# Two attention stages of a six-layer decoder kernel: fewer value products on TensorE, more copies on ScalarE, and a bias row added by GpSimd

## The reference

```python
# L0 self-attention: 16 heads of 64, one key and one value head shared by all of them
q = (x @ Wq) -> 16 heads; k, v = split(x @ Wkv)
out = softmax(q k^T / 8 + relative_bias, causal) v @ Wout + bout
# L0 cross-attention: 16 heads of 8 over ctx_1024 of the same sequence
q = x @ Wq + bq; k = ctx @ Wk + bk; v = ctx @ Wv + bv
out = softmax(q k^T / sqrt(8) + mask) v @ Wo + bo
```

## Time and profile before

| | |
|---|---|
| median of 3 runs | 2577.37 us (2576.12 to 2579.46) |
| the profiled execution | 2579.07 us |
| span of its trace | 2577.2 us |
| granted TensorE clock, mean | 0.947 |
| PE busy | 2276.2 us (88%) |
| DVE busy | 1941.7 us (75%) |
| ACT busy | 1413.3 us (55%) |
| POOL busy | 1165.4 us (45%) |

### The profile page before, as it was taken

The page is one execution under the profiler, slowest core; times in us unless marked ns, Lnnn a source line. Parts: engine busy times, 40 slices in busy tenths (PEclk is TensorE's granted clock), DMA queues, the critical chain, the costliest instruction groups (busy, mean ns, idle before and its releaser), DMA issues. The chain is left out here.

```text
span 2577.2 us, 89949 instructions
## 1 busy us (share of the span) xinstructions
PE 2276.2 (88%) x33769; PEld 1843.9 (72%) x33775; DVE 1941.7 (75%) x5469; ACT 1413.3 (55%) x3541; POOL 1165.4 (45%) x1038
## 2 busy tenths in 40 slices
PE   7999999989999871337999899998999999999975
PEld 7888888866666650126888678886888888888863
DVE  3777777758888878897888667775777777777765
ACT  1566666645665642346888678885444444444432
POOL 0333333326666642008999689994222222222222
PEclk9999999998999995758999999999999999999998
DMA  4000000000000000000000000000000000000002
GB/s 117 2 0 0 0 0 0 0 5 20 17 17 17 17 9 1 0 20 15 0 0 0 1 2 0 0 0 6 8 7 6 6 6 6 5 6 6 6 2 65
DMA packets 56164, 25.52 MB, mean 10 GB/s; under 512 B 17347, under 2 KB 55558, under 8 KB 56070
## 3 DMA queue, kind: packets, MB, share of 16 engines
q1 hardware_dynamic: 52658, 23.06, 3.3%
q10 hardware_dynamic: 3412, 1.19, 0.2%
HBM read 20.04 MB, written 4.19 MB: 9 GB/s over the span
## 5 line engine op out<-in xcount | busy, mean ns | idle before, releaser
L705 POOL TENSOR_TENSOR sa_sc<-sa_sc,sa_rs 128x1024 f32<-128x1024 f32 x64 | 121.9, 1904 | 338.0 <-DVE sa_rs L681 338.0
L1748 POOL TENSOR_TENSOR lo_qk_r<-lo_qk_ms,w_neg_half 128x20 f32<-128x20 f32 x64 | 226.9, 3546 | 22.5 <-DVE lo_qk_ms L1671 22.5
L1748 POOL TENSOR_TENSOR gl_qk_r<-gl_qk_ms,w_neg_half 128x20 f32<-128x20 f32 x64 | 226.8, 3544 | 1.1 <-DVE gl_qk_ms L1671 1.0
L947 POOL TENSOR_TENSOR xa_sc<-xa_sc,xa_rs 128x1024 f32<-128x1024 f32 x64 | 121.7, 1902 | 157.8 <-DVE xa_rs L923 157.8
L484 POOL TENSOR_TENSOR xan_ve<-xan_mv,w_eps_ln 128x1 f32<-128x1 f32 x64 | 13.3, 208 | 392.8 <-DVE xan_mv L478 392.8
L851 ACT ACTIVATE xan_xT<-xa_misc 128x128 f32<-128x128 f32 x64 | 17.8, 279 | 268.7 <-PE xa_misc L763 268.7
L784 PEld LDWEIGHTS xa_qs<-xan_xT,late_x_wq 128*128 128x128 f32 x1024 | 119.1, 191 | 52.6 <-issue 52.6
L920 DVE TENSOR_REDUCE xa_sm<-xa_sc 128x16 f32<-128x1024 f32 x64 | 78.1, 1220 | 89.2 <-ACT xa_sc L863 89.2
L678 DVE TENSOR_REDUCE sa_sm<-sa_sc 128x16 f32<-128x1024 f32 x64 | 78.1, 1220 | 82.0 <-ACT sa_sc L636 82.0
L560 PE MATMUL sa_qs<-san_xT,w_a_wq 128*128 128x128 f32 x1024 | 134.6, 286 | 1.7 <-DVE sa_sc L667 1.7
L784 PE MATMUL xa_qs<-xan_xT,late_x_wq 128*128 128x128 f32 x1024 | 131.3, 281 | 0.0
(11 more groups left out here) (330 smaller groups left out, 6833.4 us busy)
## 6 DMA issues: line engine op xcount, KB each, us to landing
w_x<-in_x_dram SPq DMA_DIRECT2D x8, 512.0 KB, 7.6
ca_cx<-in_ctx_dram SPq DMA_DIRECT2D x64, 64.0 KB, 1.8
xa_cx<-in_ctx_dram SPq DMA_DIRECT2D x64, 64.0 KB, 1.8
out_dram<-la_out SPq DMA_DIRECT2D x16, 256.0 KB, 2.3
ca_mask<-in_mask_BxSxS_ff_dram SPq DMA_DIRECT2D x64, 32.0 KB, 1.7
w_a_wq<-in_L_attn_Wq_dram SPq DMA_DIRECT2D x1, 512.0 KB
w_a_wo<-in_L_attn_Wout_dram SPq DMA_DIRECT2D x1, 512.0 KB
prep_xwo<-in_L_xattn_Wo_dram ACTq DMA_DIRECT2D x1, 512.0 KB
```

The source lines that it names most:

```text
L705: pool.tensor_tensor(v, v, bcast(rs[:, s, :], 2, S), ALU.mult).then_inc(prob_done, 1)
L947: pool.tensor_tensor(v, v, bcast(rs[:, s, :], 2, S), ALU.mult).then_inc(prob_done, 1)
L1748: pool.tensor_tensor(qk_r[:, s, :], qk_ms[:, s, :], k["neg_half"][:, 0:NQK], ALU.pow).then_inc(sg["qk_r"], 1)
```

## The change

Self: the two swapped value products go. ACT copies the values as they are, then copies each half of the rows into the other half; three activations with 64 elements in a row in place of one with 128, and the semaphore v counts three a tile.

Cross: the four value products become one over all 128 rows. ACT spreads it into both halves: four activations with 64 elements in place of two with 128. The bias row is no longer a product on PE; GpSimd adds it to x ahead of time into a new buffer `xb` (`copy_x`, lag 6, last in its order), and DVE's residual adds the output product to that.

The loops stay where the shorter or longer code ahead of them puts them. The diff, cut to the lines that change and a few around them:

```diff
@@ -537,7 +537,7 @@
                     after(pe, k_done, t, 1)
-                    after(pe, v_done, t, 1)
+                    after(pe, v_done, t, 1, per=3)
                     pe.transpose(misc[:, 0:P], norm["xn"][:, s, :], ident).then_inc(norm["xT_psum"], 1)
@@ -545,11 +545,7 @@
                     pe.matmul(misc[:, P:2 * P], k["a_wkk"][:, :, :].rearrange("p a b -> p (a b)"), xT[:, s, :], start=True, stop=True)
-                    pe.matmul(misc[:, 2 * P:2 * P + DH], xT[:, s, :], k["a_wv"][:, :], start=True, stop=True)
-                    for r in range(2):
-                        last = pe.matmul(misc[r * 64:r * 64 + 64, 2 * P + DH:3 * P], xT[:, s, (1 - r) * 64:(2 - r) * 64],
-                                         k["a_wv"][:, :], start=True, stop=True)
-                    last.then_inc(kv_psum, 1)
+                    pe.matmul(misc[:, 2 * P:2 * P + DH], xT[:, s, :], k["a_wv"][:, :], start=True, stop=True).then_inc(kv_psum, 1)
@@ -585,7 +581,7 @@
                 def attend(t, four):
-                    after(pe, v_done, t)
+                    after(pe, v_done, t, per=3)
@@ -621,7 +617,10 @@
                     after(act, o_psum, t, 4)
-                    act.activation(vx[:, four, :, :].rearrange("p a d -> p (a d)"), misc[:, 2 * P:3 * P], ACT.Copy).then_inc(v_done, 1)
+                    act.activation(vx[:, four, 0, :], misc[:, 2 * P:2 * P + DH], ACT.Copy).then_inc(v_done, 1)
+                    for r in range(2):
+                        act.activation(vx[r * 64:r * 64 + 64, four, 1, :], misc[64 - r * 64:128 - r * 64, 2 * P:2 * P + DH],
+                                       ACT.Copy).then_inc(v_done, 1)
@@ -973,6 +972,7 @@
+        xb = sb("xb", [P, 2, D])
@@ -1014,14 +1014,10 @@
-                    after(pe, v_done, t, 1, per=2)
+                    after(pe, v_done, t, 1, per=4)
                     pe.matmul(m2[:, 0:P], k["c_wq"][:, :], xcT[:, s, 0:P], start=True, stop=True)
                     pe.matmul(m2[:, P:2 * P], k["c_wk"][:, :], xcT[:, s, P:2 * P], start=True, stop=True)
-                    for b in range(2):
-                        for r in range(2):
-                            last = pe.matmul(m2[r * 64:r * 64 + 64, (2 + b) * P:(3 + b) * P], xcT[:, s, P + b * 64:P + b * 64 + 64],
-                                             k["c_wv"][:, :], start=True, stop=True)
-                    last.then_inc(qkv_psum, 1)
+                    pe.matmul(m2[:, 2 * P:3 * P], xcT[:, s, P:2 * P], k["c_wv"][:, :], start=True, stop=True).then_inc(qkv_psum, 1)
@@ -1038,7 +1034,7 @@
                 def attend(t, four):
-                    after(pe, v_done, t, per=2)
+                    after(pe, v_done, t, per=4)
@@ -1066,8 +1062,7 @@
-                    pe.matmul(m1[:, 2 * P:3 * P], oT[:, s, :], k["c_wo"][:, :], start=True, stop=False)
-                    pe.matmul(m1[:, 2 * P:3 * P], k["ones"][0:1, :], k["c_row"][0:1, :], start=False, stop=True).then_inc(y_psum, 1)
+                    pe.matmul(m1[:, 2 * P:3 * P], oT[:, s, :], k["c_wo"][:, :], start=True, stop=True).then_inc(y_psum, 1)
@@ -1096,10 +1091,10 @@
                     for r in range(2):
-                        rows = slice(r * 64, r * 64 + 64)
-                        act.activation(vz[rows, four, :, :, :].rearrange("p b c (q w) -> p b (c q) w", q=2)[:, :, :, r * HD:r * HD + HD],
-                                       m2[rows, 2 * P:4 * P].rearrange("p (b n e d) -> p b n e d", b=2, e=2, d=HD)[:, :, :, r, :],
-                                       ACT.Copy).then_inc(v_done, 1)
+                        for b in range(2):
+                            act.activation(vz[r * 64:r * 64 + 64, four, b, :, :].rearrange("p c (q w) -> p (c q) w", q=2)[:, :, r * HD:r * HD + HD],
+                                           m2[b * 64:b * 64 + 64, 2 * P:3 * P].rearrange("p (n e d) -> p n e d", e=2, d=HD)[:, :, r, :],
+                                           ACT.Copy).then_inc(v_done, 1)
@@ -1146,8 +1141,10 @@
                 def residual(t, four):
+                    s = four % 2
                     after(dve, y_psum, t)
-                    dve.tensor_tensor(tile_of(X, t), m1[:, 2 * P:3 * P], tile_of(X, t), ALU.add).then_inc(x_done, 1)
+                    after(dve, xb_done, t)
+                    dve.tensor_tensor(tile_of(X, t), m1[:, 2 * P:3 * P], xb[:, s, :], ALU.add).then_inc(x_done, 1)
@@ -1174,7 +1171,11 @@
-                skewed(pool, NT, [(4, shift), (0, rsqrt), (2, blocks)], 4)
+                def copy_x(t, four):
+                    after(pool, x_done, t, 2)
+                    pool.tensor_tensor(xb[:, four % 2, :], tile_of(X, t), k["c_row"][:, :], ALU.add).then_inc(xb_done, 1)
+
+                skewed(pool, NT, [(4, shift), (0, rsqrt), (2, blocks), (6, copy_x)], 4)
```

More of the change, by code:

```diff
@@ L987, in narrow_cross_attention @@
                                                               sem("outT_psum"), sem("inverse"), sem("outT"))
-        y_psum, x_done = sem("y_psum"), sem("x")
+        y_psum, xb_done, x_done = sem("y_psum"), sem("x_plus_bias"), sem("x")
         with nc.Block() as block:
```

## The result

The changed kernel takes 2551.78 us (median of three runs, 2550.27 to 2557.35) where the kernel before took 2577.37: ratio 0.9907, 95% interval [0.9893, 0.992]. The forecast was 2558.5. Its profiled execution is the one of 2550.27, with a span of 2548.5 us and a mean granted clock of 0.947, as before.

What follows compares the result with a forecast made beforehand. PE bound self-attention; a 5.70 us ring of waits bound narrow cross-attention. Self -16 and cross -3 gave -19, 2579.07 to 2560.0 profiled, and 2558.5 for the median, 1.7 lower; own range 2554 to 2563, stated range 2549 to 2572.

Steps and rivals of the forecast that it cites:

- rival 1: Cross: the four value copies overlap, so the GpSimd ring sets 5.50 us; -12 there, total -28, 2549 us; chance 0.13.
- rival 2: Cross: the four value copies cost as much each as now, 1.14 us; total -6, 2571 us; chance 0.12.
- Self, -16: Self-attention: removing L550's products takes 0.26 us a tile off full PE, over 62 tiles -16 us.
- ACT's longer queue: Self: three copies make ACT 0.4 us later a tile, hidden behind PE's other work, so no cost.
- Cross, -3: Narrow cross-attention: period falls from 5.70 to 5.65 us, -0.05 over 60 tiles, -3 us.
- Bias row -0.41: Cross: without the bias row's product on PE the residual is released 0.41 us earlier a tile.
- the forecast's +0.36: Cross: four value copies of 64 elements take 0.93 us where two of 128 took 0.57.
- ring one: Cross: waits from bias addition through attend, value copies, turned, output product and residual; sets 5.70 us a tile, forecast 5.65.
- Ring two: Cross: waits through GpSimd's shift and DVE's apply, 5.50 us a tile; catches the gain if the first ring gets shorter.
- rival 4: Cross: GpSimd's add is dear, at 1.04 us the period is 6.00; +18, total +2, 2579 us; chance 0.04.
- rival 3: Self: the saving does not come, since query weight loads that L550 hid come out; total -3, 2574 us; chance 0.06.
- Rival 5: Loops fetch an instruction page anew at some 13 turns, 1.35 us each; +18, 2576 us; chance 0.04.

Runs made afterwards that it cites:

- e7: Changed kernel with the two half-height value products of self-attention issued again, results unused; 2568.94 us, ratio 0.9969 to the kernel before.
- e12: Kernel before with only cross's one value product, four copies and counts of four, plus 185 idle-stretch semaphore instructions to keep code placement; 2588.48 us, ratio 1.0047.
- e2: Kernel before with only the cross-attention part of the change, self as before; 2570.04 us, ratio 0.997.
- e3: Kernel before with only the narrow cross-attention's bias row moved to GpSimd; 2657.92 us, ratio 1.0322.
- e4: Kernel before with the two value copies counting 2 each and TensorE's waits counting fours, no work moved; 2575.33 us, ratio 0.9997.
- e11: Changed kernel, placed as e9, with ScalarE's four cross value copies behind the copy of the turned tile; 2538.55 us, ratio 0.9847 to the kernel before.
- e9: Changed kernel with 84 semaphore instructions on TensorE in the feed-forward's idle stretch, moving later code; 2547.83 us, ratio 0.9884 to the kernel before.
- e10: Kernel before with 192 semaphore instructions on TensorE in the feed-forward's idle stretch, moving later code; 2670.94 us, ratio 1.036.
- 165 and 172: Kernels whose last wide cross-attention loop lies 165 or 172 instructions, modulo 256, from its place in the kernel before; profiles stall at 3, 1 and 0 of 13 turns.
- e5: Changed kernel with 84 semaphore instructions on TensorE just ahead of the last wide cross-attention; 2554.5 us, ratio 0.9922 to the kernel before.
- e6: Kernel before with 172 semaphore instructions on TensorE just ahead of the last wide cross-attention; 2626.46 us, ratio 1.0202.

## Why the prediction was right, and where not

**The total: in the range, in part by luck.** 25.6 us came off and 18.9 were forecast. The measured 2551.78 lies under the forecast's own range of 2554 to 2563; it is inside the stated one because that was widened for rival 1, overlapping copies, which did not come. In the stages the miss was larger, 36.5 for 19, and the stall, of the other sign, hid 7.4 of it. The chances do not add either: what is counted as faster comes to 0.80 (0.55, 0.13 and all of rival 2's 0.12), not 0.82.

**Self, -16: right in mechanism, a term too small.** The stage gave 25.4. The forecast took L550's own time, 0.26 from its start to its successor's; the pair costs 0.41 with what it adds to its neighbours, as e7 shows by putting it back. 62 x 0.41 would be 25; the loop's turn takes 0.07 a tile of it back (7.53 on average and not 7.46), so the tiles give some 21, as the stretch between the residuals has it at like clock (488.8 to 467.6). The other 4 came with 7 us less at 1.2 GHz, which no part of the sum had and the change cannot claim: the self code of before, in the other kernels here, has heads of 29.9 us (e12) to 33.6 (e2), with 6.8 to 16.4 us at 1.2 GHz. So the saving was mis-sized by some 5 us and the rest is clock. That ACT's longer queue would cost nothing held.

**Cross, -3: the links were right, one was missed, and the base was a single tile.** Bias row -0.41, copies +0.37 for the forecast's +0.36, the copies not overlapping and no dearer: these steps measured as priced, and e12 and e3 show them apart. What failed is "ring one becomes 5.70 - 0.41 + 0.36 = 5.65". The 5.70 is one tile of four; the four are 5.88, 5.78, 5.70 and 5.80, 5.79 on average, and the check over the whole stage was pulled down to 5.70 by its fast ends. In the steady part the average went from 5.79 to 5.65. And the wait ahead of attend fell by 0.10, from counts that became fours (e4). That 5.65 was hit to the digit is luck: the base was 0.09 too low, and the missed link gave 0.10 back. Between the first residual and the last the stage is 8.2 shorter; the other 2.9 lie ahead of the first one, where TensorE had 13.8 us at 1.2 GHz for 20.5.

**Ring two at 5.50 held** where it was made to bind, in e11. The add on GpSimd was 0.46 for 0.40 and hidden, so rival 4 falls with rivals 1 and 2, and rival 3 falls with the self saving. On rival 1: the Trainium skill (ScalarE: Activation LUTs, What ACT_TABLE_LOAD costs) would give the four copies 0.68, and the row has 0.94; the measurement decides, they do not overlap.

**The other stages, priced at nothing: wrong by +7.4.** Rival 5 had the mechanism, at 1.35 us a turn; a turn that fetches costs 6.7 to 7.0. The 1.35 was the time of a packet on the DMA engines, from a share rounded to 0.2%, and no row shows that an engine waits that long and for one packet: nine come, and a part of the 6.7 is the half clock behind the wait. It was looked for in the loops that the change shortens, but it struck in the longest loop of the kernel, which is only moved. For the profiled execution the forecast was 2560.0 and it took 2550.27: the two changed stages gave 17.5 more than forecast, and this took 7.4 back. The trace of before had no sign of it, and the sign after is one line: 69 packets for 61, with less code. The Trainium skill (Runtime: NRT & Kernel Launch, Instruction fetch mechanics) says that a taken branch stalls when its target lies outside a window of two blocks, and also that TensorE, unlike most engines, holds 2,048 instructions, which is eight blocks. The traces of before and e9 disagree with two blocks and agree with eight: their loop of 1,598 instructions a turn, over six blocks, comes round 13 times without a packet. e3 and e10 agree with the stall, though their loop is as long. Such a loop touches seven or eight blocks according to its place; whether that decides was not tested, and it would not explain why 165 and 172 stall only now and then. Why 9 packets come at some places of the code and none at others stays open.

## What to carry to other kernels

Take a period over whole loop turns in the steady part, not from one tile and not over ramps, and read the granted clock of the ramps before a stage's difference is given to the change; and price a removed instruction by the starts of its neighbours on both sides, since a pair that held PE for 0.26 us gave back 0.41. When a change alters the amount of code ahead of a long loop, compare the instruction queue's packets and that loop's time before and after, even where the loop isn't touched: here the same loop cost between 0 and 91 us more by its place alone, and a part of a change tried by itself (e3) looked 3% slower for that reason only. A removed link pays until the next ring: one place further on the four value copies were off ring one, but only 0.15 of their 0.94 us came off the tile (5.65 to 5.50).

## What the runs showed of the hardware

- The place of a long loop in TensorE's program decides whether each return waits about 7 us and brings 9 packets of 16.4 KB (before and e9 against e3 and e10): 722 or 814 us for the same 64 tiles.
- After such a wait the granted clock is 0.50 for a while: 0.50 from 1913 to 1916 us in the changed kernel.
- The same stage code had 6.8 us (e12) to 16.4 us (e2) at 1.2 GHz in its head, and took 29.9 to 33.6 us for it.
- Increments of a semaphore by TensorE, 84 (e5) or 172 (e6) in a row, start 0.15 us apart; they made the stage 0.12 to 0.14 us longer each.
- fp32 value products of 64 columns cost some 0.2 us each at half height as at full height (0.41 for two, 0.23 for one).
- One more wait instruction on TensorE behind the last release costs 0.11 us (705.16 to 705.27 in the kernel before): the product starts 0.25 us after the release, against 0.15 with one wait instruction (e4).
- Copies by ScalarE of 64 partitions by 64 elements from PSUM take 0.22 to 0.24 us each, one behind the other.
